# A router step of a three-layer megakernel: small VectorE instructions moved to GpSimd, one copy placed between two VectorE steps

## The reference

```python
x = x + 0.5 * ffn(layernorm(x))
x = x + attn(layernorm(x))
x = x + 0.5 * ffn(layernorm(x))
```

```python
scores = einsum('bhqd,bhkd->bhqk', Q, K) / sqrt(16)
thresh = top_k(scores, 31)[0][..., -1:]
attn = softmax(where(scores < thresh, -inf, scores))
```

```python
logits = normalize(h) @ normalize(sim) - sigmoid(gates)
gated = relu(logits)
# a token with no positive logit falls back on its two largest ones
mask = (logits > 0) or, where none is, top_2(logits)
rw = softmax(where(mask, gated, -inf))
q, k, v = sum over e of rw[e] * (h @ {q,k,v}_proj[e])
att = softmax(causal(q @ k.T / 8)) @ v
out = sum over e of (att * rw[e]) @ o_proj[e]
```

## Time and profile before

| | us |
|---|---|
| median of three runs | 4385.38 |
| lowest, highest | 4381.74, 4391.22 |
| profiled execution, its time | 4391.22 |
| its span, from first to last instruction | 4389.4 |

### The profile page before, as it was taken

How to read it: one execution, slowest core, us unless ns; L and a number is a source line. 1 busy time by engine, 2 the same in 40 slices (tenths; PEclk the granted TensorE clock), 3 DMA queues, 4 the chain that set the end, 5 groups by cost and what they waited for, 6 DMA issues and landing times.

```text
span 4389.4 us, 93568 instructions
## 1 busy us (share of the span) xinstructions
PE 3853.7 (88%) x29004; PEld 3142.2 (72%) x29004; DVE 4068.6 (93%) x14510; ACT 3579.3 (82%) x9797; POOL 3502.4 (80%) x3927
## 2 busy tenths in 40 slices
PE   6777889998998999899899989989998998987777
PEld 5556777777777777777777777777777777765566
DVE  2389999999999999999999999999999999999992
ACT  2378889888888988888888888888988888888772
POOL 1467888888888888888888888988889898876650
PEclk8788999999999999999999999999999999998877
DMA  3111112121212121121212121121212122110111
GB/s 106 40 32 35 53 56 55 52 58 53 59 53 57 53 58 52 54 58 54 58 51 59 53 58 54 52 58 53 59 52 59 52 58 52 53 46 23 29 31 53
DMA packets 243941, 230.47 MB, mean 53 GB/s; under 512 B 27123, under 2 KB 176628, under 8 KB 243316
## 3 DMA queue, kind: packets, MB, share of 16 engines
q1 hardware_dynamic: 243444, 224.49, 18.5%
HBM read 214.98 MB, written 9.44 MB: 51 GB/s over the span
## 4 chain that ended last, share of the span: by engine, by line
DVE 60%; PE 20%; POOL 12%; ACT 5%; issue 2%; DMA 1%; SPq 0%; POOLq 0%; ACTq 0%; DVEq 0%
DVE M L986 9%; DVE HL L988 8%; PE pQ L642 7%; DVE HL L1003 5%; DVE HL L1011 5%; DVE HL L1017 4%; DVE HL L1007 4%; DVE M L1005 4%; DVE HL L1009 4%; DVE M L1019 4%; DVE M L1015 4%; DVE HL L1013 4%; DVE M L1001 4%; POOL HS L394 2%; POOL S L1071 2%
## 5 line engine op out<-in xcount | busy, mean ns | idle before, releaser
L642 PE MATMUL pQ<-wf_sb,HS 128*128 128x192 f32 x8192 | 1457.4, 332 | 68.7 <-POOL HS L394 47.1
L642 PEld LDWEIGHTS pQ<-wf_sb,HS 128*128 128x128 f32 x8192 | 1359.9, 194 | 104.1 <-issue 84.8
L874 ACT ACTIVATE S<-S,M 128x512 f32<-128x512 f32 x1024 | 799.9, 781 | 4.4 <-DVE M L986 1.4
L881 ACT ACTIVATE S<-S,lift 128x512 f32<-128x512 f32 x1024 | 787.2, 769 | 2.1 <-POOL lift L1060 2.1
L860 ACT COPY S<-pST 128x256 f32<-128x256 f32 x768 | 308.9, 402 | 332.7 <-issue 292.1
L394 POOL TENSOR_TENSOR HS<-hT_a,RB 128x1024 f32<-128x1024 f32 x244 | 578.6, 2371 | 0.0
L394 POOL TENSOR_TENSOR HS<-hT_b,RB 128x1024 f32<-128x1024 f32 x240 | 568.8, 2370 | 4.2 <-PE pQ L642 2.4
L869 ACT COPY PTs<-pST 128x512 f32<-128x512 f32 x1024 | 529.5, 612 | 7.7 <-PE pST L661 7.1
L1069 POOL TENSOR_TENSOR HL<-S,HL 128x512 f32<-128x512 f32 x384 | 491.2, 1279 | 50.6 <-ACT HL L862 50.1
L661 PE MATMUL pST<-ident,S 128*128 128x128 f32 x4096 | 508.2, 279 | 15.2 <-ACT S L857 12.7
L1071 POOL TENSOR_TENSOR S<-HL 128x512 f32<-128x512 f32 x384 | 493.8, 1286 | 30.1
(11 more groups left out here) (251 smaller groups left out, 8838.3 us busy)
## 6 DMA issues: line engine op xcount, KB each, us to landing
RB<-rows_b SPq DMA_DIRECT2D x384, 256.0 KB, 3.4
RB<-rows_a SPq DMA_DIRECT2D x384, 256.0 KB, 3.4
x_b<-in_x SPq DMA_DIRECT2D x64, 128.0 KB, 3.1
out_y<-y SPq DMA_DIRECT2D x64, 128.0 KB, 1.7
wf_sb<-in_wf SPq DMA_DIRECT2D x4, 768.0 KB, 7.1
rows_b<-rwT SPq DMA_DIRECT2D x64, 8.0 KB, 1.3
wof_sb<-in_wof SPq DMA_DIRECT2D x1, 1024.0 KB, 7.1
rows_a<-rwT SPq DMA_DIRECT2D x64, 8.0 KB, 1.3
```

The source lines that it names most:

```text
L642: mm = nc.tensor.matmul(pQ[:, 0:QKV], HS[:, k % 2, e, i, :], wf_sb[:, i, at:at + QKV], start=k + e + i == 0, stop=(k, e, i) == (3, 3, 1))
L874: nc.scalar.activation(S[:, r, :], S[:, r, :], ACT.Prelu, bias=M8[:, r, TH:TH + 1], scale=-1.0, alpha=1.0 / STEEP).then_inc(s_cut, 1)
L881: nc.scalar.activation(S[:, r, :], S[:, r, :], ACT.Exp, bias=lift[:, r:r + 1], scale=-STEEP).then_inc(s_gap, 1)
```

## The change

Four things are changed, all in the router and the softmax of both `ffn` jobs.

1. `top` on VectorE is only the `MAX8`. The copy of the two largest to `mr8` becomes a step of its own, `pair`, a copy on GpSimd one slot later (slot 4 for job `a`), and the match becomes `repl` on VectorE, again a slot later. The engine that used to make the copy now waits for another one.
2. The negative of max(largest, 0) is made by GpSimd, as a fifth small instruction of `gate`, and so the waits on `gate`'s semaphore count by five.
3. The reciprocal of the gate's sum leaves VectorE and stands in `rw` on GpSimd, as a power with exponent -1. The step `gate_rec` has no slot of its own any more.
4. The reciprocal of the softmax's sum (`sc_rec`) moves to GpSimd in the same slot, also as a power, and stands there behind `hs` and ahead of `mix`. `sc_norm` is one slot earlier.

`gate`, `gate_exp`, `gate_em` and `gate_sum` are two slots later for both jobs; `rw` keeps its slot. At the ends, where VectorE does the router itself, it does the new steps too, with its own reciprocal (`inverse`).

```diff
-        "hT": 79, "h_rinv": 79, "lg": 81, "shift": 82, "top": 83, "gate": 85,
-        "gate_exp": 86, "gate_em": 87, "gate_sum": 88, "gate_rec": 89, "rw": 91, ...
+        "hT": 79, "h_rinv": 79, "lg": 81, "shift": 82, "top": 83, "pair": 84, "repl": 85, "gate": 87,
+        "gate_exp": 88, "gate_em": 89, "gate_sum": 90, "rw": 91, ...
...
+        def inverse(ends, out, of):
+            if ends:
+                return nc.vector.reciprocal(out[:], of[:])
+            return nc.gpsimd.tensor_tensor(out[:], of[:], minus_one[:, 0:1], ALU.pow)
...
+            if at := mine("pair"):
+                t, c = at
+                wait(eng, q["top"], t + 1)
+                ns.tensor_copy(J.mr8[:, 0:2], J.v8[:, 0:2]).then_inc(q["pair"], 1)
             if at := mine("gate"):
...
-                wait(eng, g, 4 * t + 3)
+                ns.tensor_scalar(J.nv[:], J.v8[:, 0:1], 0.0, -1.0, ALU.max, ALU.mult).then_inc(g, 1)
+                wait(eng, g, 5 * t + 4)
...
             if at := mine("rw"):
                 t, c = at
+                wait(eng, q["gate_sum"], t + 1)
+                inverse(ends, J.rgs, J.gs).then_inc(q["gate_rec"], 1)
                 wait(eng, q["gate_rec"], t + 1)
...
+            if at := mine("sc_rec"):
+                t, c = at
+                wait(eng, q["sc_exp"], t + 1)
+                inverse(ends, J.rrs, J.rs).then_inc(q["sc_rec"], 1)
...
                 if at := tile(J, "top", w, j):
                     t, c = at
                     wait(dve, q["shift"], t + 1)
-                    nc.vector.max(J.v8[:, 0:8], J.L[:]).then_inc(q["top"], 1)
-                    dve.wait_ge(q["top"], t + 1)
-                    nc.vector.tensor_reduce(J.mr8[:, 0:2], J.v8[:, 0:2].unsqueeze(2), mybir.AxisListType.X, ALU.max
-                                            ).then_inc(q["pair"], 1)
-                    nc.vector.tensor_reduce(J.nv[:], J.v8[:, 0:16:8], mybir.AxisListType.X, ALU.max, negate=True
-                                            ).then_inc(q["guard"], 1)
-                    dve.wait_ge(q["pair"], t + 1)
+                    nc.vector.max(J.v8[:], J.L[:]).then_inc(q["top"], 1)
+                if at := tile(J, "repl", w, j):
+                    t, c = at
+                    wait(dve, q["pair"], t + 1)
                     nc.vector.match_replace(J.R[:], J.mr8[:], J.L[:], -BIG).then_inc(q["repl"], 1)
-                if at := tile(J, "gate_rec", w, j):
-                    t, c = at
-                    dve.wait_ge(q["gate_sum"], t + 1)
-                    nc.vector.reciprocal(J.rgs[:], J.gs[:]).then_inc(q["gate_rec"], 1)
-                if at := tile(J, "sc_rec", w, j):
-                    t, c = at
-                    dve.wait_ge(q["sc_exp"], t + 1)
-                    nc.vector.reciprocal(J.rrs[:], J.rs[:]).then_inc(q["sc_rec"], 1)
```

More of the change, by code:

```diff
@@ L62 @@
         "ctx_rec": 69, "ctx_norm": 71, "ctxT": 72, "x": 74, "x_sq": 76, "x_rstd": 77, "h": 78,
-        "hT": 79, "h_rinv": 79, "lg": 81, "shift": 82, "top": 83, "gate": 85,
-        "gate_exp": 86, "gate_em": 87, "gate_sum": 88, "gate_rec": 89, "rw": 91, "rwT": 92, "rw_st": 93, "hs": 96, "qkv": 104,
-        "qkT": 105, "sc": 107, "sc_max": 107, "sc_exp": 110, "sc_rec": 111, "sc_norm": 113,
+        "hT": 79, "h_rinv": 79, "lg": 81, "shift": 82, "top": 83, "pair": 84, "repl": 85, "gate": 87,
+        "gate_exp": 88, "gate_em": 89, "gate_sum": 90, "rw": 91, "rwT": 92, "rw_st": 93, "hs": 96, "qkv": 104,
+        "qkT": 105, "sc": 107, "sc_max": 107, "sc_exp": 110, "sc_rec": 111, "sc_norm": 112,
         "pT": 114, "rb2": 114, "attT": 116, "mix": 117, "y": 119, "out": 120,
@@ L69 @@
         "x_ld": -51, "x_sum": -48, "x_sq": -46, "x_rstd": -45, "h": -44, "hT": -43, "h_rinv": -43,
-        "lg": -41, "shift": -40, "top": -39, "gate": -36, "gate_exp": -35,
-        "gate_em": -34, "gate_sum": -33, "gate_rec": -32, "rw": -30, "rwT": -29, "rw_st": -28, "hs": -24, "qkv": -16, "qkT": -15,
-        "sc": -14, "sc_max": -13, "sc_exp": -10, "sc_rec": -9, "sc_norm": -7, "pT": -6,
+        "lg": -41, "shift": -40, "top": -39, "pair": -38, "repl": -37, "gate": -34, "gate_exp": -33,
+        "gate_em": -32, "gate_sum": -31, "rw": -30, "rwT": -29, "rw_st": -28, "hs": -24, "qkv": -16, "qkT": -15,
+        "sc": -14, "sc_max": -13, "sc_exp": -10, "sc_rec": -9, "sc_norm": -8, "pT": -6,
         "rb2": -6, "attT": -4, "mix": -3, "y": 0, "y_sq": 3, "y_rstd": 4, "y_norm": 5, "xn": 8,
@@ L257, in __init__ @@
                     sb(f"{k}_{n}", P, E) for k in ("Lr", "L", "R", "fb", "fb2", "pos", "ep", "eg", "em", "rw"))
-                self.v8 = sb(f"v8_{n}", P, 16)
+                self.v8 = sb(f"v8_{n}", P, 8)
                 self.mr8 = sb(f"mr8_{n}", P, 8)
@@ L271, in __init__ @@
                     "full", "read", "x_in", "x_sum", "x_sq", "x_eps", "x_rstd", "x_bias", "h_norm", "h_sq",
-                    "h_guard", "h_rinv", "shift", "top", "pair", "guard", "repl", "gate", "gate_exp", "gate_em", "gate_sum",
+                    "h_guard", "h_rinv", "shift", "top", "pair", "repl", "gate", "gate_exp", "gate_em", "gate_sum",
                     "gate_rec", "rw", "rw_st", "sc_max", "sc_exp", "sc_rec", "sc_norm")}
@@ L324, in at_end @@
                 return t < TPB
-            return t >= TILES - (3 if key in ("hs", "mix") else 2)
+            return t >= TILES - (3 if key in ("hs", "sc_rec", "mix") else 2)
         def power(eng, ns, src, v1, v2, op1, op2, guarded, out, exponent, guard_ready, out_ready, t):
@@ L366, in layer @@
                 if ends:
-                    wait(eng, g, 4 * t)
+                    wait(eng, g, 5 * t)
                 eng.wait_ge(q["repl"], t + 1)
@@ L377, in layer @@
                 ns.tensor_tensor(J.ep[:], J.eg[:], J.pos[:], ALU.mult).then_inc(q["gate_em"], 1)
-                wait(eng, q["gate"], 4 * t + 4)
+                wait(eng, q["gate"], 5 * t + 5)
                 eng.wait_ge(q["gate_em"], 2 * t + 1)
@@ L724, in ffn @@
                     t, c = at
-                    act.wait_ge(q["gate"], 4 * t + 4)
+                    act.wait_ge(q["gate"], 5 * t + 5)
                     nc.scalar.activation(J.eg[:], J.L[:], ACT.Exp, bias=J.nv[:]).then_inc(q["gate_exp"], 1)
@@ L925, in _ @@
                 nc.vector.memset(jobs[n].mr8[:], BIG)
-                nc.vector.memset(jobs[n].v8[:], 0.0)
             nc.vector.memset(keep[:, 0:1], 0.0)
```

## The result

The changed kernel takes 4585.1 us (median of four runs, 4581.81 to 4590.6), the kernel before beside it 4385.26 us (four runs, 4381.74 to 4391.22). The ratio is 1.0456, interval 1.0437 to 1.0473: slower by 200 us, where 124 were forecast (4509). It lies in the given range, at its upper end. The profiled execution took 4587.97 us with a span of 4586.2, so 196.8 us more than the profiled execution before.

What follows compares the result with a forecast made beforehand. VectorE, 98.4% busy, and a chain leaving it and returning at `nm_a` were taken to set the pace nearly together. The terms gave +9.05 us per four tiles, 124 us over 55 tiles: 4509 us, range 4405 to 4600.

Steps and rivals of the forecast that it cites:

- The new wait: GpSimd's copy waits for `v_a` ahead of `mix`: y later by 4.45 us in three tiles of four, 1.0 in one.
- The slack of `Sr`: At `nm_a`, `Sr` was ready early in one tile, taking 0.77 us off the delay over four tiles.
- The reciprocals in VectorE's part of the chain: Two reciprocals leave VectorE's part of the chain, taking 4 x 0.13 us off four tiles.
- The clock's give-back: On TensorE, y and scores may regain full clock: up to 8.1 us less in four tiles, middle taken.
- What would show it: Signs: `nm_a` waits 150 us or more, VectorE about 95% busy, y 10.3 us behind `v_a`, four tiles about 264 us.
- A: Rival: VectorE's relief counts, the tile shrinks by 0.84 us, 46 us in all, to 4339 us; chance 0.12.
- B: Rival: GpSimd's added work becomes the bound; a tile 1 us longer gives +55 us, 4440 us; chance 0.12.
- C: Rival: restored clock and more slack in `Sr` cancel the shift, within 9 us of 4385; chance 0.04.

Runs made afterwards that it cites:

- e1: Changed kernel with both jobs' copies of the two largest back on VectorE, one slot behind `top`: 4338.18 us, ratio 0.9882.
- e3: Changed kernel with only job b's copy back on VectorE, job a's still on GpSimd: 4585.77 us, ratio 1.0447.
- e4: Changed kernel with both copies still on GpSimd but one slot later, job a's behind the split: 4345.48 us, ratio 0.9898.
- e7: Kernel before plus only a GpSimd wait for job a's `top` and an unused copy in slot 4: 4673.83 us, ratio 1.0659.
- e5: Changed kernel with GpSimd's copy at its slot's end, behind `HS` and statistics, ahead of the split: 4399.91 us, ratio 1.0035.
- e8: Kernel before with only the two reciprocals moved to GpSimd as powers: 4392.73 us, ratio 1.0015.
- e6: Changed kernel plus 20 unused transposes on TensorE ahead of its wait for job a's `mix`: 4516.67 us, ratio 1.03.
- e10: e1 plus 20 unused transposes on TensorE ahead of its wait for job a's `mix`, as a control: 4342.06 us, ratio 0.9894.
- e9: e4 plus 20 unused transposes on TensorE ahead of its wait for job a's `mix`: 4333.56 us, ratio 0.9877.

## Why the prediction was right, and where it missed

*The new wait*: right. Place, mechanism and amount held: the lag of y behind `v_a` is 10.3 us in every kind of tile, and the leg grew by 14.65 us in four tiles where 3 x 4.45 + 1.0 = 14.35 was forecast. e1 to e3 show whose copy it is, e4 that the place and not the work costs, e7 that the wait does it without any other part of the change. Over e4, e5, after and e7 the lag in three tiles of four goes 5.9, 6.7, 10.3, 11.4 us, and four tiles take 252.1, 255.9, 268.3, 274.5: from e5 to after the sum of the lags grows by 12.7 us and the four tiles by 12.4. There each microsecond at the copy comes back at `nm_a`. The two outer steps cost more than their lag (2.8 us of lag and 3.8 of time from e4 to e5, 4.5 and 6.2 from after to e7); the rest stands between y and `Sr`.

*The slack of `Sr`*: 0.77 us was counted and 1.25 taken up (1.4 to 0.1 in the table's last leg): better by 0.5.

*The reciprocals in VectorE's part of the chain*: -0.52 us was counted for four tiles, and +0.09 came. The price of 0.06 each was right (e8), but the match of job b moved into this leg with the change: between `nm_a` at 2629.00 and the search at 2629.35 now stand its two rows, 0.15 us. I counted what left the leg and not what came into it.

*The clock's give-back*: this is the term that was mis-sized. I took the middle of nothing and 8.1 us, a gain of 4.05 in four tiles; y to `Sr` grew by 0.3 instead. The middle rested on "Two standings instead of one make either as likely", for which I had no row. Of 48 tiles y ran at full clock (2.1 us or less) in 11 before and in 7 after, and took over 3.4 us in 24 before and 30 after. Stretches of after in the tile shown, from L658 to behind y; they answer to the earlier trace rows:

```profile
2662.40:2663.60 1.20, 1.20 (x8) 1.20 (x9) 1.20 (x3) 1.20 (x4) 1.01 (x4) 1.00 0.12 44
2663.60:2667.00 3.40, 3.02 (x10) 2.52 (x8) 3.40 (x10) 2.68 (x7) 3.32 (x3) 0.50 0.18 61
2667.10:2670.40 3.30, 0.58 (x3) 0.56 (x4) 3.30 (x11) 0.00 (x0) 3.13 (x4) 1.00 0.00 0
2670.50:2673.80 3.30, 3.30 (x10) 1.92 (x13) 3.30 (x15) 0.00 (x0) 3.30 (x4) 0.50 0.00 0
```

The granted clock fell twice. After the first standing L658 began at 1.00 and went on at 0.50 from 2663.60; it needs 4.29 us here (2.77 in the earlier trace rows). During the second standing the clock was back at 1.00, y still began with it at 2669.82, and from 2670.42 on y and the start of the scores ran at 0.50. So the earlier standing did put a slow stretch onto L658, but it gave y nothing, for a second one followed. The Trainium skill (TensorE: Matmul & The Clock Gate, "HAM oscillation — how this bites in real kernels") describes a kernel in which a long wait for a DMA lies between bursts of products, and the slow clock is paid for once in every round. In this tile the rows agree in kind, with two waits for GpSimd and two slow stretches; in the one at 2603.79, where y took 1.97 us behind 2.46 us of standing, they do not. Two slow stretches were what I named as the upper end and then halved.

Put together: forecast +9.05 in four tiles, measured +13.76; the clock makes 4.3 of the 4.7 between them, lag and reciprocals 0.3 and 0.6 more, the slack 0.5 less. Times 55 / 4 that is 65 us of the 73 by which the profiled sum was too low; the other 8 are what the 196.8 us have over the table's 189, and were not followed further.

*What would show it*: the lag and GpSimd's wait at the copy held, and `nm_a` waits in every tile. Four tiles take 268 us where 264 were forecast. VectorE's waits at `nm_a` are 135.6 us, not 150, and its busy share 92.4%, not 95%: 119 us of its standing came as waits for splits [first block of waits after], which I had not forecast. All of those lie between `v_a` and `nm_a`, and `nm_a` still starts 0.03 us behind the end of `Sr` in each of the 48 tiles, so they take from its wait and do not add to the tile.

*The rivals.* A, that VectorE's relief counts: false for this change, and true only in part one step away. VectorE's own work, four tiles less its waits, is 254.5 - 3.9 = 250.7 us before and 252.1 - 4.7 = 247.4 in e4, so the 0.84 us a tile of the forecast is there; in e4 the chain still hides most of it. Of the 2.4 us that e4 has less in four tiles, 0.9 are the lag, all of it the fourth tile's (9.3 to 8.3 us, where the gate's four instructions have left the place ahead of `mix`), 0.5 the leg from y to `Sr`, and 1.1 the last leg (1.4 to 0.3), in which `nm_a` used to wait for VectorE itself: no more than this last is the relief's. e1 has next to none of the relief and is 50 us under the kernel before beside it, by fewer waits. The Trainium skill (Perfetto Trace Analysis, "Identifying the Most-Contended Engine") would relieve the busiest engine first; here that engine was relieved and the kernel lost 4.6%. With the wait out of GpSimd's way (e4), at most 1.1 of the 3.3 us that four tiles were relieved of showed in the time. B is excluded by e4, C by the size.

What stays open: why the same standing of 2.4 us ahead of y leaves the clock high once (2603.79, 1.97 us) and low another time (2871.55, 3.50 us). The standing just before does not decide alone; I did not try to separate the earlier ones. The moved slots were never run alone either: e1 and e4 have them and are faster than the kernel before, and e7 has the loss without them. Nor was it tried whether e4's copy with only some of the other moves does better.

## What to carry to other kernels

A small step that moves to another in-order engine brings its wait along, and everything queued behind it there waits too: read how far ahead of the producer that engine runs at this place (here 5 us), and add up what stands behind. If the step has to move, put it at the first place that the engine reaches after the producer; here one slot made the difference between +4.6% and -1.0%. And count a leg of the chain anew after a move, with what comes into it as well as what leaves it.

## What the hardware showed beyond that

- Twenty small transposes in the place of a standing of some 3 us kept TensorE at 2.4 GHz: y took 1.99 us in the tile shown, 3.18 in the one of after, worth 68 us on a kernel bound by this chain (e6) and nothing on one bound by VectorE (e10). Where TensorE had stood only 0.5 us, they made y 1.5 us later (e4 to e9, fourth tile).
- A VectorE copy of 128x2 that began inside a GpSimd product or split ended 0.02 to 0.03 us behind it, in 36 of 36 cases of e1, and took up to 2.26 us instead of 0.15; a reduction of the same two values took 0.15 to 0.16 us there (before, 71 of 71). The profile calls VectorE busy meanwhile.
- A power of one value takes GpSimd 0.54 to 0.58 us and a user right behind it starts 0.1 us later, where VectorE's reciprocal costs that engine 0.06. In e8 that exchange was a small loss.
- VectorE at 98.4% busy was not the bound. At 99.8% (e1) it was, with waits of 7.0 us in 3380, and 40 us of that were copies that stood.
